# Re-timing one batch's normalisations, q projection and rotation inside a hand-ordered attention kernel

## The chip, the cores and the metric

The kernel runs on one core of one Trainium2 chip. Its engines are TensorE (PE in the profile, with its weight loads as PEld), VectorE (DVE), ScalarE (ACT), GpSimd (POOL) and SyncE (SP), which here only issues transfers. The metric is the device time of one execution in microseconds; a lower time is better.

## The reference

One pre-norm transformer layer without learned norm weights, on x of shape (8, 512, 128), all float32:

```python
x = x + attention(layernorm(x))      # 16 heads of 8 columns, rotary q and k, causal softmax
x = x + experts(layernorm(x))        # 8 experts, tokens chosen by top-k of Sinkhorn-normalised gates

q, k, v = split(xn @ W_attn)
q = q * cos + rotate_half(q) * sin   # the same for k
att = softmax(where(causal, q @ k.T / sqrt(8), -inf))
y = (att @ v) @ W_proj
```

## The kernel before

There are eight batches of 512 tokens, each kept as four tiles of 128 tokens. Attention goes through the batches in turn, and each batch through four **slots** of four heads; slot (b, s) below is slot s of batch b. In a slot, every engine goes through the same list, each taking the entries that are its own:

```python
STEP = [("w", 8), ("n", 0), ("n", 1), ("v", 0), ("u", 0), ("w", 9), ("x", 0), ("u", 1), ("u", 2),
        ("v", 3), ("u", 3), ("mx", 0), ("v", 1), ("v", 2), ("u", 4), ("c", 0), ("x", 1), ("u", 5),
        ("c", 1), ("u", 6), ("c", 2), ("x", 2), ("u", 7), ("c", 3), ("c", 4), ("c", 5), ("x", 3),
        ("ot", 0), ("c", 6), ("u", 8), ("c", 7), ("u", 9), ("x", 4)]
```

- `u0` to `u9`: score rows of the **next** slot (PE, L470); DVE takes the row maxima (L937).
- `n0`, `n1`: DVE turns the sixteen maxima of this slot into minus the maximum as a high and a low bf16 part, in NMX (L948, L951). Each is a tiny instruction.
- `mx`: PE transposes NMX (L516), ACT copies it into the rows of q (L695, "the take of mx"). No chunk of the slot can start before.
- `c0` to `c7`, and `w8`, `w9` at the start of the following slot: PE makes a chunk of transposed scores (L483), ACT takes the exponential (L735), and POOL zeroes what causality forbids (L860, `causal`). c0 and c2 have no `causal` of their own, and the others give eight of them a slot, counted z0 (c1), z1 (c3), z2 to z5 (c4 to c7), z6 (w8), z7 (w9). Chunk c6 waits for the exponential of c3, c7 for that of c4, w8 for that of c5.
- `v0`, `v3`, `v1`, `v2`: PE multiplies the previous slot's exponentials with the values (L495). v0 waits for z1, v3 and v1 for z5, v2 for z7.
- `ot` in slots 0 and 2: PE transposes the result (L503), DVE divides by the sums (L958, L963).
- `x0` to `x4`: places for other work, filled by the table EXTRAS.

The other work of a batch: `xnT` (PE transposes the normalised tiles XN, ACT copies them to XNT), `q`, `k`, `v` (projections, L527 and L535), `yT`, `proj`, `xn2T`, `logits`. After `q` or `k`, DVE makes the **turn** (L929 multiplies with cosines, L930 shuffles into TS), POOL multiplies TS with sines (L840, the **product**) and adds TC (L844, the **sum**), and the result RES is cut into three bf16 parts: ACT rounds (L729, `cut`), POOL subtracts (L848, `subtract`), and so on. SP stores the parts to DRAM (L362) and loads them back as rows of q and k (L369) for the next batch's scores. All of this goes through a single PSUM bank MB (`xnT`, `q`, `k`, `v`, `mx`, `ot`, `yT`, `proj`, `xn2T`, `logits`), which the users take strictly in the order of the list: each waits until its predecessor has been copied out.

The tables give places as (slot, kind, index), and the last number of an entry says for which batch the work is, counted from the running one. For batch 0, entries ending in 2 are kept and the others are replaced by tables FIRST_.... `normalize_x` (POOL, L832) makes tiles of XN with one instruction each, `normalize_x2` (ACT, L713) tiles of the second norm, XN2, also one instruction each, and `rstd` (POOL, L816 to L823) the scale factors that the latter needs.

Of the kernel before, what the change touches and what calls it, by code (L numbers as in the profile page):

```python
# [52 lines left out]


EXTRAS = {(0, 1): ("k", 1), (1, 1): ("yT", -1), (1, 2): ("proj", -1), (1, 3): ("v", 1),
          (2, 4): ("xnT", 2), (3, 0): ("q", 2), (3, 1): ("xn2T", -1), (3, 2): ("logits", -1)}
TURN = [i ^ 16 for i in range(32)]
ROTATE = {(3, "u", 2): (0, 2), (0, "c", 4): (1, 1)}
CUT = {(3, "c", 1): (0, 0, 2), (0, "x", 0): (0, 1, 1), (0, "c", 1): (0, 2, 1),
       (1, "x", 0): (1, 0, 1), (1, "v", 1): (1, 1, 1), (1, "c", 1): (1, 2, 1)}  # L60
SUBTRACT = {(3, "c", 5): (0, 0, 2), (0, "u", 2): (0, 1, 1), (1, "u", 2): (1, 0, 1), (1, "u", 3): (1, 1, 1)}
NORMALIZE = {(2, "u", 1): (0, 3, 2), (2, "c", 4): (3, 4, 2)}
PART_ORDER = [(0, 0), (0, 1), (0, 2), (1, 0), (1, 1), (1, 2)]

# [97 lines left out]
def build(nc, x_in, w_qkv, w_swap, w_proj, gate_w, experts, rope, tri, ident, small, out):  # L162
    ctx = ExitStack()
    with ctx:
# [643 lines left out]
        def _(pool):  # L808
# [25 lines left out]
                if hi == TB:  # L834
                    last.then_inc(xn_ready, 1)

            def rotate(w, b):
                pool.wait_ge(misc_free, BANK_TURN["qk"[w], b] + 1)
                pool.nop(nofuse=True)
                pool.tensor_tensor(TS[w][:, :], TS[w][:, :], ROPE[:, 2 * w + 1, :], ALU.mult)  # L840
                pool.drain()
                if not (isinstance(b, int) and b == 0):
                    pool.wait_ge(part[w], 3 * b)
                pool.tensor_tensor(RES[w][:, :], TC[w][:, :], TS[w][:, :], ALU.add).then_inc(resid[w], 1)  # L844
# [51 lines left out]
            for j, (b, t) in enumerate(order):  # L896
                x = X[:, TB * b + t, :]
# [408 lines left out]
```

## Time and profile before

| what | value |
|---|---|
| median of 3 runs | 486.92 us (485.73 to 487.55) |
| profiled execution, its time | 488.2 us |
| profiled execution, its span from first to last instruction | 486.5 us |
| time outside the span | 1.7 us |
| slots (3,0), (3,1), (3,2), (3,3), from n0 to n0 | 10.39, 10.77, 9.21, 11.58 us |
| slot (6,2), which has no xnT and no normalisation of x | 9.21 us |

The four slots of a batch repeat almost to the hundredth from batch 1 to batch 5, so times are given on the clock of batch 3 (175.04 to 216.99 us of the span) unless another is named. A row of the timeline has the start, the duration, the engine, the line, the operation with its tiles and shapes, and in brackets the idle time of the engine before it and what ended it.

### The profile page before, as it was taken

The numbers are of one execution on the slowest core, as the hardware profiler recorded it, in microseconds if no ns is written. First come the engines' busy times: TensorE is split into PE (matmuls) and PEld (weight loads), VectorE is DVE, ScalarE is ACT, GpSimd is POOL, SyncE is SP. The second block draws the span as 40 slices with busy tenths as digits, with TensorE's granted clock in tenths as the row PEclk, the third lists the DMA queues.
The fourth block names the chain that finished last, engine by engine and source line by source line (L and its number), as shares of the span: only waits on it lengthen the run. The fifth ranks groups of instructions, "written<-read, shape, count | busy, mean of one in ns | idle before, by whom it ended". The sixth has DMA issues, their size and how long they took to land.

```text
span 486.5 us, 9335 instructions
## 1 busy us (share of the span) xinstructions
PE 409.0 (84%) x2799; PEld 203.8 (42%) x2799; DVE 403.2 (83%) x1630; ACT 306.1 (63%) x599; POOL 245.1 (50%) x425
## 2 busy tenths in 40 slices
PE   5458887988989899898989989899999878999563
PEld 4233343444435445444544544455444433434121
DVE  6978766888798888888888888898897776996997
ACT  1002584878678787867878786788778331533871
POOL 3142773667565747766665676554344200000895
PEclk9955988999999999999999999999999977999998
DMA  8670044126117022511702341170001010100122
GB/s 256 214 183 1 34 132 96 56 77 130 55 46 165 21 84 90 112 54 67 163 6 84 104 94 59 62 164 23 2 0 64 4 44 0 44 23 22 44 65 86
DMA packets 28435, 36.85 MB, mean 76 GB/s; under 512 B 2145, under 2 KB 24225, under 8 KB 26913
## 3 DMA queue, kind: packets, MB, share of 16 engines
q1 hardware_dynamic: 27312, 34.68, 25.6%
q10 hardware_dynamic: 1072, 1.57, 1.1%
q8 instruction: 22, 0.36, 0.3%
q14 instruction: 29, 0.23, 0.2%
HBM read 19.41 MB, written 16.78 MB: 74 GB/s over the span
## 4 chain that ended last, share of the span: by engine, by line
PE 53%; DVE 15%; ACT 9%; POOL 8%; issue 7%; POOLq 3%; DMA 3%; SPq 1%; DVEq 0%; ACTq 0%
PE PVB L495 12%; PE ROWB L470 10%; PE CHB L483 8%; ACT YS L735 7%; PE MB L535 5%; POOL YS L860 4%; PE ROWB L627 3%; PE CHB L627 3%; PE MB L527 3%; POOL XN L832 3%; PE MB L503 3%; DVE YS L1227 2%; DVE CHB L1227 2%; DVE X L1233 2%; PE ROWB L680 2%
## 5 line engine op out<-in xcount | busy, mean ns | idle before, releaser
L937 DVE CUSTOM_DVE_ANT_0 JUNK<-ROWB,TRI 128x384 bf16<-128x384 f32 (+3 forms) x512 | 220.5, 484 | 41.7 <-PE ROWB L470 40.0
L735 ACT ACTIVATE YS<-CHB 128x512 f32<-128x512 f32 x320 | 172.9, 612 | 36.9 <-PE CHB L483 36.2
L860 POOL TENSOR_SCALAR_AFFINE_SELECT YS<-YS 128x256 f32<-128x256 f32 x256 | 102.1, 408 | 117.9 <-ACT YS L735 111.7
L470 PE MATMUL ROWB<-YS 96*128 96x384 bf16 (+3 forms) x512 | 122.3, 312 | 8.2 <-DVE MX L937 2.9
L483 PE MATMUL CHB<-YS 104*128 104x384 bf16 (+3 forms) x512 | 116.3, 303 | 14.7 <-ACT YS L735 13.7
L495 PE MATMUL PVB<-YS,VP 128*32 128x512 f32 (+3 forms) x1024 | 94.1, 442 | 6.8 <-POOL YS L860 6.4
L470 PEld LDWEIGHTS ROWB<-YS 96*128 96x128 bf16 x512 | 43.1, 100 | 83.7 <-DVE MX L937 47.9
L695 ACT ACTIVATE YS<-MB 8x1024 bf16<-8x1024 bf16 x32 | 32.5, 1016 | 63.0 <-PE MB L516 63.0
L483 PEld LDWEIGHTS CHB<-YS 104*128 104x128 bf16 x512 | 44.2, 98 | 46.5 <-ACT YS L735 26.3
L495 PEld LDWEIGHTS PVB<-YS,VP 128*32 128x32 f32 x1024 | 34.3, 109 | 34.5 <-POOL YS L860 22.2
L899 POOL TENSOR_TENSOR SUM<-YS 128x512 f32<-128x512 f32 x10 | 13.0, 1301 | 61.6 <-ACT YS L803 61.6
L937 DVE DVE_READ_ACCUMULATOR2_ANT MX<- 128x1 f32 x512 | 41.9, 82 | 0.0
L627 PE MATMUL CHB<-WEXP,XS 128*128 128x512 f32 x64 | 34.9, 654 | 7.8 <-DVE X L1233 7.8
L848 POOL TENSOR_TENSOR RES<-RES,PARTS 128x512 f32<-128x512 f32 x28 | 32.4, 1162 | 8.1 <-ACT PARTS L729 7.8
L627 PE MATMUL ROWB<-WEXP,XS 128*128 128x512 f32 x56 | 29.3, 639 | 3.5 <-DVE X L1233 3.5
L803 ACT ACTIVATE YS<-YS,W 128x128 f32<-128x128 f32 x80 | 24.1, 388 | 5.8 <-POOL SUM L899 4.1
L729 ACT ACTIVATE PARTS<-RES 128x512 bf16<-128x512 f32 x42 | 26.5, 631 | 0.7 <-POOL RES L848 0.5
L783 ACT ACTIVATE YS<-CHB 128x1024 f32<-128x1024 f32 x10 | 10.2, 1023 | 21.6 <-PE CHB L627 21.6
L840 POOL TENSOR_TENSOR TS<-TS,ROPE 128x512 f32<-128x512 f32 x14 | 17.9, 1279 | 8.6 <-DVE TS L930 8.6
L832 POOL TENSOR_SCALAR XN<-X,MV,RSTD 128x128 f32<-128x128 f32 x28 | 22.1, 795 | 0.2 <-issue 0.2
L783 ACT ACTIVATE YS<-ROWB 128x1024 f32<-128x1024 f32 x10 | 10.2, 1023 | 18.1 <-PE ROWB L627 18.1
L627 PEld LDWEIGHTS CHB<-WEXP,XS 128*128 128x128 f32 x64 | 11.6, 203 | 21.4 <-issue 21.3
(134 smaller groups left out, 514.2 us busy)
## 6 DMA issues: line engine op xcount, KB each, us to landing
YS<-parts_scratch SPq DMA_DIRECT2D x28, 384.0 KB, 7.0
parts_scratch<-PARTS SPq DMA_DIRECT2D x15, 384.0 KB, 2.4
parts_scratch<-PARTS SPq DMA_DIRECT2D x15, 256.0 KB, 2.1
X<-in_x SPq DMA_DIRECT2D x8, 256.0 KB, 5.0
xn_scratch<-XN2S SPq DMA_DIRECT2D x8, 256.0 KB, 2.0
XS<-xn_scratch SPq DMA_DIRECT2D x8, 256.0 KB, 2.7
out<-X SPq DMA_DIRECT2D x8, 256.0 KB, 2.3
parts_scratch<-PARTS SPq DMA_DIRECT2D x15, 128.0 KB, 1.7
```

What stands on the lines that cost most here:

```text
L470: last = pe.matmul(ROWP[BANK[u]][:, col:col + keys], QP[par][0:ROWS_K, pair, P * qb:keys], KZ[par][i % 2][0:ROWS_K, pair, 0:keys], start=T ...
L483: last = pe.matmul(CH[BANK[c]][:, col:col + n], KZ[par][i % 2][0:ALL_K, pair, P * kb:P * kb + P], QP[par][0:ALL_K, pair, P * kb:T], start= ...
L495: last = pe.matmul(PVB[32 * i:32 * i + 32, P * kb:T], VP[par][:, v:v + 32], PT[s % 2][:, c, col:col + T - P * kb], start=(kb == 0 and s % ...
L535: last = pe.matmul(MB[:, n * t:n * t + n], src[:, P * t:P * t + P], weight, start=True, stop=True)
L627: last = pe.matmul(buffer(n, half), XS[b % 2][:, P * t:P * t + P], WEXP[:, 4 * half:4 * half + 4, :].rearrange("p e o -> p (e o)"), start= ...
L695: act.activation(dst, src, ACT.Copy).then_inc(misc_free, 1)
L729: act.activation(PARTS[w][:, i, :], RES[w][:, :], ACT.Copy).then_inc(part[w], 1)
L735: act.activation(PT[s % 2][:, c, :], CH[BANK[c]], ACT.Exp).then_inc(exp_done, 1)
L832: last = pool.tensor_scalar(XN[:, t, :], X[:, n, :], MV[:, n, 0:1], RSTD[:, n:n + 1], ALU.subtract, ALU.mult)
L848: pool.tensor_tensor(RES[w][:, :], RES[w][:, :], PARTS[w][:, i, :], ALU.subtract).then_inc(resid[w], 1)
L860: pool.affine_select(out=v, in_=v, pattern=[[0, 2], [1, P]], compare_op=ALU.is_ge, fill=0.0, base=0, channel_multiplier=-1).then_inc(causa ...
L937: last = dve.tensor_tensor_reduce(out=JUNK[BANK[u]][:, col:col + n], in0=ROWP[BANK[u]][:, col:col + n], in1=TRI[:, T - n:T], scale=1.0, sc ...
```

## The change

Six parts, all of them places in the tables or the order of one engine's steps:

1. `xnT` of batch b+2 goes from the end of slot 2 (x4) to x1 of slot 2; `q` of b+2 from x0 of slot 3 to x2 of slot 2.
2. `normalize_x` for b+2, four tiles on POOL: from slot 2 (three after u1, one after c4) to two after z5 of slot 0 and two after z5 of slot 1.
3. `rotate` is split in `sine_product` and `rotate`. For q of b+2: product after c5 and sum after c7 of slot 2 (both were after u2 of slot 3). For k of b+1: product after c2 and sum after c4 of slot 0 (both were after c4). In batch 0 both stay where they were.
4. The first cut of q goes from c1 of slot 3 to v1 of slot 3, just behind the take of mx on ACT; the second from x0 of the next slot 0 to c4 of slot 3.
5. The first subtraction of q goes from c5 to c1 of slot 3, the second from u2 of the next slot 0 to c5 of slot 3.
6. `normalize_x2`: its four ACT instructions go from slot 2 (two after c1, two after c6) to just behind w9 of slot 3, ahead of the take of mx.

```diff
-          (2, 4): ("xnT", 2), (3, 0): ("q", 2), (3, 1): ("xn2T", -1), (3, 2): ("logits", -1)}
+          (2, 1): ("xnT", 2), (2, 2): ("q", 2), (3, 1): ("xn2T", -1), (3, 2): ("logits", -1)}
 TURN = [i ^ 16 for i in range(32)]
-ROTATE = {(3, "u", 2): (0, 2), (0, "c", 4): (1, 1)}
-CUT = {(3, "c", 1): (0, 0, 2), (0, "x", 0): (0, 1, 1), (0, "c", 1): (0, 2, 1),
+PRODUCT = {(2, "c", 5): (0, 2), (0, "c", 2): (1, 1)}
+ROTATE = {(2, "c", 7): (0, 2), (0, "c", 4): (1, 1)}
+CUT = {(3, "v", 1): (0, 0, 2), (3, "c", 4): (0, 1, 2), (0, "c", 1): (0, 2, 1),
        (1, "x", 0): (1, 0, 1), (1, "v", 1): (1, 1, 1), (1, "c", 1): (1, 2, 1)}
-SUBTRACT = {(3, "c", 5): (0, 0, 2), (0, "u", 2): (0, 1, 1), (1, "u", 2): (1, 0, 1), (1, "u", 3): (1, 1, 1)}
-NORMALIZE = {(2, "u", 1): (0, 3, 2), (2, "c", 4): (3, 4, 2)}
+SUBTRACT = {(3, "c", 1): (0, 0, 2), (3, "c", 5): (0, 1, 2), (1, "u", 2): (1, 0, 1), (1, "u", 3): (1, 1, 1)}
+NORMALIZE = {(0, "c", 7): (0, 2, 2), (1, "c", 7): (2, 4, 2)}
...
+FIRST_PRODUCT = {(0, "c", 4): (0, 1), (0, "x", 4): (1, 1)}
 FIRST_ROTATE = {(0, "c", 4): (0, 1), (0, "x", 4): (1, 1)}
...
-NORMALIZE2 = {(2, "c", 1): (0, 2), (2, "c", 6): (2, 4)}
+NORMALIZE2 = {(3, "w", 9): (0, 4)}
...
-            def rotate(w, b):
+            def sine_product(w, b):
                 pool.wait_ge(misc_free, BANK_TURN["qk"[w], b] + 1)
                 pool.nop(nofuse=True)
                 pool.tensor_tensor(TS[w][:, :], TS[w][:, :], ROPE[:, 2 * w + 1, :], ALU.mult)
+
+            def rotate(w, b):
                 pool.drain()
                 if not (isinstance(b, int) and b == 0):
                     pool.wait_ge(part[w], 3 * b)
...
+                        if (s, kind, i) in PRODUCT_OF[bt.b]:
+                            sine_product(*PRODUCT_OF[bt.b][s, kind, i])
                         if (s, kind, i) in ROTATE_OF[bt.b]:
                             rotate(*ROTATE_OF[bt.b][s, kind, i])
```

On POOL an entry's own `causal` comes first, then product, sum, subtraction and normalisation of the same place.

## Rows read from the trace of the kernel before

**Rows 1.** Busy time by slot: (3,2) and (3,3).
```profile
core 0: us, PE busy (x) PEld busy (x) DVE busy (x) ACT busy (x) POOL busy (x), PEclk, DMA share, GB/s
196.20:205.41 9.21, 7.72 (x73) 4.28 (x74) 8.03 (x37) 7.93 (x17) 7.79 (x16) 1.00 0.48 108
205.41:216.99 11.58, 10.94 (x91) 5.29 (x90) 8.98 (x38) 8.04 (x15) 6.21 (x10) 1.00 0.16 58
```

**Rows 2.** Timeline of PE, slots (3,2) and (3,3).
```profile
198.01 1.24 PE L495 MATMUL PVB<-YS,VP 128*32 128x384 f32 x13
...
199.41 0.38 PE L483 MATMUL CHB<-YS 104*128 104x512 bf16 x1
...
202.44 0.61 PE L503 MATMUL MB<-IDF,OT 128*128 128x128 f32 x4
...
204.59 0.63 PE L503 MATMUL MB<-IDF,XN 128*128 128x128 f32 x4 [0.66 <-POOL XN L832]
205.06 0.39 PE L483 MATMUL CHB<-YS 104*128 104x256 bf16 x2
...
206.60 0.38 PE L483 MATMUL CHB<-YS 104*128 104x256 bf16 x2
206.82 1.02 PE L527 MATMUL MB<-XNT,WQKV 128*128 128x512 f32 x2
...
209.34 0.22 PE L516 MATMUL MB<-IDB,NMX 128*8 128x128 bf16 x1 [0.39 <-DVE TS L930]
...
211.18 0.60 PE L503 MATMUL MB<-IDF,XN 128*128 128x128 f32 x4
```

**Rows 3.** Timeline of ACT, slots (3,2) and (3,3).
```profile
200.80 0.87 ACT L713 ACTIVATE XN<-X,SHIFT,RSTD 128x128 f32<-128x128 f32 x2
201.57 2.54 ACT L735 ACTIVATE YS<-CHB 128x512 f32<-128x512 f32 x5
...
207.02 0.60 ACT L735 ACTIVATE YS<-CHB 128x512 f32<-128x512 f32 x1 [0.67 <-PE CHB L483]
209.76 1.02 ACT L695 ACTIVATE YS<-MB 8x1024 bf16<-8x1024 bf16 x1 [2.15 <-PE MB L516]
211.38 0.60 ACT L735 ACTIVATE YS<-CHB 128x512 f32<-128x512 f32 x1 [0.60 <-PE CHB L483]
211.88 0.60 ACT L695 ACTIVATE XN2S<-MB 128x512 f32<-128x512 f32 x1
```

**Rows 4.** Timeline of DVE: n1 of slot (0,1), then slots (3,2), (3,3).
```profile
55.55 1.20 DVE L951 SCALAR_TENSOR_TENSOR NMX<-MX,NMX 128x16 bf16<-128x16 f32 x1
...
196.51 0.18 DVE L951 SCALAR_TENSOR_TENSOR NMX<-MX,NMX 128x16 bf16<-128x16 f32 x1
...
203.09 0.36 DVE L958 RECIPROCAL RSUM<-MB 128x32 f32<-128x32 f32 x1 [0.52 <-PE MB L503]
...
207.95 0.69 DVE L929 TENSOR_TENSOR TC<-MB,ROPE 128x512 f32<-128x512 f32 x1 [0.34 <-PE MB L527]
```

**Rows 5.** POOL: slot (0,1), end of (3,0), a norm's group, PE's wait.
```profile
55.44 1.27 POOL L840 TENSOR_TENSOR TS<-TS,ROPE 128x512 f32<-128x512 f32 x1
...
185.89 1.84 POOL L860 TENSOR_SCALAR_AFFINE_SELECT YS<-YS 128x256 f32<-128x256 f32 x5
...
L832 POOL TENSOR_SCALAR XN<-X,MV,RSTD x28: 789/792/812, 36.6 to 287.8; 128x128 f32<-128x128 f32 x28
...
187.07 0.43 PE L495 MATMUL PVB<-YS,VP 128*32 128x128 f32 x8 [1.01 <-POOL YS L860]
```

**Rows 6.** Start-up: timeline of PE in slots (0,3) and (1,0).
```profile
80.13 0.43 PE L470 MATMUL ROWB<-YS 96*128 96x512 bf16 x1 [2.26 <-issue]
...
85.88 0.38 PE L483 MATMUL CHB<-YS 104*128 104x512 bf16 x1
...
91.22 0.39 PE L470 MATMUL ROWB<-YS 96*128 96x512 bf16 x1
...
94.59 0.38 PE L483 MATMUL CHB<-YS 104*128 104x512 bf16 x1
```

More of the change, by code:

```diff
@@ L85 @@
 EXTRAS_OF = planned(EXTRAS, FIRST_EXTRAS)
+PRODUCT_OF = planned(PRODUCT, FIRST_PRODUCT)
 ROTATE_OF = planned(ROTATE, FIRST_ROTATE)
```

## The prediction

> **What bounds the kernel now.** I read the busy times of the page first: PE 84% and DVE 83% of the span, ACT 63%, POOL 50%. Neither of the first two is a plain bound, so the place of the idle time counts. The second view is busy time by slot. Slot (3,3) lasts 11.58 us for 8.98 us of DVE, 2.60 us idle, while slot (3,2) lasts 9.21 us for 8.03 [rows 1]. The third is the timeline of each engine across those two slots, which says what slot 3 waits for. There are two things. The transposes `xnT` at the end of slot 2 stand on PE until POOL has made the fourth tile (0.66 us) and push w8, v0 and u0 back, so that DVE has nothing between n1 and its first row maximum. Then `q` takes 1.02 us of PE, the turn takes DVE, and `mx` waits for the turn because it shares MB: it starts at 209.34, 1.39 us after L929 began [rows 2, 4]. ACT sits idle 2.15 us before it can take mx, and c0's exponential comes at 211.38, 5.97 us after n0 at 205.41 [rows 1, 3]. From there ACT sets the slot's end: w8 waits for the exponential of c5, and v0 and the next u0 stand behind w8.
>
> **The turn in slot 2 (parts 1 and 3).** I follow the new chain from c0 on PE to the n0 of slot 3, with delays taken from the rows. xnT starts 0.22 us after c0. ACT's take comes 0.70 us later (211.18 to 211.88) and lasts 0.60; q starts 0.05 after it. L929 starts 1.13 us after q (206.82 to 207.95). `ot` must now wait for the turn as mx did, 1.39 us. DVE's reciprocal follows ot by 0.65 us (202.44 to 203.09), and n0 follows the reciprocal by 2.32 us (203.09 to 205.41). The sum is 0.22 + 0.70 + 0.65 + 1.13 + 1.39 + 0.65 + 2.32 = 7.06 us, where before it is 6.00 us (199.41 to 205.41) [rows 1 to 4]. Slot 2 gets **1.06 us** longer.
>
> **POOL's norms ahead of slot 2 (part 2).** Each slot now has 2 x 0.79 = 1.58 us of `normalize_x` right behind z5, in front of z6 and z7 [rows 5]. This costs in two ways. First, z7 is later and v2 waits for it: z5 had ended just before n1's 196.51, and 1.58 us of norms and z6 and z7 (0.36 + 0.41) bring z7's end to about 198.8, while v2 is the last eight of the thirteen matmuls from 198.01 to 199.25 and began near 198.5 [rows 2, 4, 5]. That is 0.3 us. Second, n1. Its duration is 0.18 us alone, but in slot (0,1) it started at 55.55 inside a POOL product of 55.44 to 56.71 and lasted to 56.75 [rows 4, 5]. I take it that a POOL instruction in flight holds n0 and n1 until it ends. In slot (3,2) n1 began at 196.51, just behind z5; now a norm will be in flight until 197.21, so n1 ends near 197.23 instead of 196.69, u0 is 0.48 us late, and u3, mx, v1, v2 and c0 with it. The two costs overlap, so I take **0.47 us**; the bounds are 0.3 (only z7) and 1.3 (n0 and both norms in a row, should n0 come a little later).
>
> The Trainium skill (SBUF — State Buffer, "SBUF: two separate sides") has such a rule: the port pair that DVE and GpSimd share is an exclusive lock, held for a whole instruction, and it asks for a DVE operation with two SBUF inputs or a two-port mode and a GpSimd operation that reads SBUF. The trace agrees with it in n1's 1.20 us. By the rule the norms would block as the product did, which gives the 0.48 us; without it part 2 would cost the 0.3 us of z7 alone.
>
> **Slot 3 without q (parts 1, 4, 6).** After `ot` PE goes through c6, u8, c7, u9 to w8, an estimate of 0.44 + 4 x 0.22 = 1.32 us by the pace of w9 and q (206.60 and 206.82), and w9's exponential follows w8 by 1.96 us (205.06 to 207.02). As ot is 2.97 us ahead of n0, that exponential starts 0.31 us after n0. Behind it stand the four norms of part 6: the exponential's 0.48, then 4 x 0.385 (200.80 to 201.57 for two) = 1.54 us. So the take of mx starts 2.33 us after n0; mx itself would be ready some 0.4 us sooner, so the norms cost that much. c0's exponential follows the take by 1.62 us (209.76 to 211.38). The first cut of q falls into this gap, which had 0.60 us idle for a pitch of 0.52: no cost. c0's exponential is then 3.95 us after n0 where it was 5.97: **2.02 us** gained [rows 2, 3]. Between c0 and c5 there is one cut as before (the second, instead of the first), which leaves the gain of 2.02, less what was hidden: the take of xn2T and the logits keep their places, and PE's c1 to c3 now follow the take of xn2T as before, but cut 1 at c4 comes after PE's wait for the logits, where cut 0 at c1 was covered by it (c1 had 0.48 us of room before c2 was needed). So 0.48 us is paid that was hidden: **1.54 us** net at c5. Were the cut covered after all, it would be 2.02.
>
> POOL at the same place: z3, then one subtraction of q, then z4 and z5 for the next v3, as before; the other subtraction now lies behind z0, ahead of the wait for c3's exponential. No change. On SP nothing moves: it stores q's parts behind the save of XN2S, as before.
>
> Slots 2 and 3 together: + 1.06 + 0.47 - 1.54 = -0.01 us a batch.
>
> **Slots 0 and 1 (parts 2 and 3).** Product and sum of k stood in one row after z2, z3 to z7 followed only from 185.89 on, and v3 of slot (3,1) waited 1.01 us for z5 [rows 5]. The product at c2 lies in POOL's wait for c3's exponential, so z3 to z7 start some 1.25 us sooner (184.64) and z5 ends at 185.77. That gain is spent again: two norms hold n1 until about 186.55, where the causals held it to 186.3, and u3 must wait for u0, so mx comes 0.2 us sooner, not 1.0; z7 ends at 185.77 + 1.58 + 0.72 = 188.07 instead of 185.89 + 1.84 = 187.73; k's first subtraction follows it, and the cut behind that stands on ACT ahead of c0's exponential. Gain and loss nearly cancel there: **-0.07 us**; bounds -0.4 (norms hidden) and +0.3 (z7 and the cut both late). A batch in full is thus -0.08, and five of them (1 to 5) **-0.4 us**.
>
> **Batch 0.** In slot (0,0) two norms now stand ahead of k's rotation at x4; the chain of cuts behind it moves by about 1.0 us (1.58 less 0.5 us of room), and the loads for batch 1 too. u0 of slot (0,3), which waits for those loads after 2.26 us of idle PE, moves from 80.13 to about 81.1. The longer slot 2 is hidden in that wait. But from u0 to c0 PE took 5.75 us with q (80.13 to 85.88) and takes 3.37 us without (91.22 to 94.59) [rows 6]; there is no second norm in this batch. + 1.0 - 2.4 = **-1.4 us**; bounds -2.4 (the norms are covered) and 0 (the chain moves by all of 1.58, and PE is slow again after its wait).
>
> **Batches 6 and 7.** No xnT, q or norms of x are left. Slot (6,2) lasts 9.21 us like (3,2) (the table ahead): there the norms of ACT delay c2's exponential and so c5 and ot, and DVE stands 0.52 us before the reciprocal [rows 4]. Without them this idle time goes, and slot 3 pays 0.1 as PE is early there. -0.4 us in each batch. Batch 6 also has the earlier product without norms behind it, so half of v3's wait of 1.01 us goes (u3 then waits for u0): -0.5 us. Together **-1.3 us**.
>
> **Sum.** -0.4 - 1.4 - 1.3 = -3.1 us against the profiled execution's 488.2 us (span 486.5 plus 1.7). Taken from the median of 486.92 this is 483.8; I say **483.9 us**.
>
> **The rivals.**
>
> *The sum catches n1 in slot 3.* By the same rows, q's sum (1.27 us) after c7 is dangerous. I put z5's end at 207.02, n0 at 206.94 and the sum at 207.15. If n0 starts after z5's end, n1 finds the sum in flight and u0 moves by 1.1 us. mx comes that much later, of which ACT's norms hide 0.4 to 0.5: + 0.6 us in five batches, + 3.0, which gives **486.9 us**. The distance is 0.1 us, less than my error, but the instant behind z5, in which the queue drains, favours n1. Chance 0.2. The rule of the Trainium skill just named would make it so whenever the sum takes the pair first, and would give this time.
>
> *Start-up brings nothing*, since the delayed chain of k's cuts decides there (the bound of 0 above): **485.3 us**. For: everything in slot (0,1) hangs on that chain. Against: the 2.4 us are read from two slots that differ by q. Chance 0.1.
>
> *Slower.* n1 is caught as above and nothing hides it: ACT is behind in slot 3 anyway because the four norms, two cuts and the exponentials stand in one row, so all 1.15 us reach c5, 5 x 1.15 = 5.8 us: 483.9 + 5.8 = **489.7 us**. It decides once ACT has no idle time left ahead of the take of mx; against it stands the 2.15 us of idle time there before [rows 3]. Chance 0.13.
>
> *The change doesn't do what it says*: q's cuts earlier could bring loads forward, but k's cuts come last in SP's order and keep their places, so this is neither gain nor loss and no case of its own.
>
> *As summed*, chance 0.57, between 481.5 and 485.5: each batch may be off by 0.3 us.
>
> **How the numbers follow.** This kernel's measurement tells 0.5%, or 2.4 us, from no change, so faster means below 484.5. The summed case puts about 0.42 of its 0.57 there and the rest within. Same takes that rest, the first rival and start-up: 0.44. Slower takes its rival and a little more: 0.14. The range from 481.5 to 488.5 leaves out the slower case and a larger gain. The likeliest case's own range is 481.5 to 485.5.
>
> **What the profile would show.** Slot (3,2) near 10.7 us, slot (3,3) near 9.6 and ACT's idle time before its take of mx near zero in slot 3; n1 near 0.7 us in slots 1 and 2; n1 of slot 3 at 0.2 or, for the first rival, above 1.2; PE's wait before v3 in slot 1 gone; slot (0,3) shorter by more than 4 us, most of it moved into (0,2). The prediction is wrong if `ot` does not wait for the turn, or if n1 is not held by norms.

## The result, and the profile after

| what | before | after |
|---|---|---|
| median of 6 runs each | 486.62 us (485.73 to 487.55) | 490.06 us (488.79 to 491.28) |
| ratio to before, 95% interval | | 1.0072 (1.0051 to 1.0094) |
| profiled execution, its span | 488.2, 486.5 us | 489.57, 487.8 us |

The changed kernel is 0.7% slower, 3.44 us by the medians. Lines moved: n0 and n1 are now L955 and L958, row maxima L944, the turn's shuffle L937, chunks L486, scores L473, values L498, transposes L506 and L519, exponentials L738, the take of mx L698, cuts L732, second norm L716, `causal` L865, norms L835, product L843, sum L849, subtractions L853, loads L372.

Busy time by slot of batch 3, from n0 to n0, for the changed kernel (the columns of [rows 1]):

```profile
175.68:186.57 10.89, 10.24 (x85) 4.67 (x77) 9.92 (x41) 7.93 (x15) 6.70 (x13) 1.00 0.07 24
186.57:197.43 10.86, 10.00 (x86) 5.54 (x87) 9.21 (x43) 8.90 (x19) 7.04 (x13) 1.00 0.48 128
197.43:208.32 10.89, 10.00 (x81) 4.82 (x81) 9.43 (x40) 7.55 (x14) 7.98 (x16) 1.00 0.45 95
208.32:218.52 10.20, 8.46 (x76) 4.65 (x77) 8.58 (x36) 8.76 (x17) 5.07 (x10) 1.00 0.22 78
```

Slot (3,2) went from 9.21 to 10.89 us, slot (3,3) from 11.58 to 10.20 [rows 1], slot (3,0) from 10.39 to 10.89 and (3,1) from 10.77 to 10.86. DVE is busier in slot (3,0) than before (9.92 us for 9.42), although its list did not change there: busy time holds waiting too. The rows of DVE and POOL around n0 and n1 say what for. First DVE of the changed kernel, at n0 and n1 of slots (3,1), (3,3) and (4,0):

```profile
186.57 0.43 DVE L955 TENSOR_SCALAR NMX<-MX 128x16 bf16<-128x16 f32 x1
187.03 0.21 DVE L958 SCALAR_TENSOR_TENSOR NMX<-MX,NMX 128x16 bf16<-128x16 f32 x1
...
208.32 0.18 DVE L955 TENSOR_SCALAR NMX<-MX 128x16 bf16<-128x16 f32 x1
208.53 1.28 DVE L958 SCALAR_TENSOR_TENSOR NMX<-MX,NMX 128x16 bf16<-128x16 f32 x1
...
218.52 0.87 DVE L955 TENSOR_SCALAR NMX<-MX 128x16 bf16<-128x16 f32 x1
```

Then POOL at the same places:

```profile
185.84 1.13 POOL L865 TENSOR_SCALAR_AFFINE_SELECT YS<-YS 128x256 f32<-128x256 f32 x3
186.96 1.59 POOL L835 TENSOR_SCALAR XN<-X,MV,RSTD 128x128 f32<-128x128 f32 x2
...
189.25 1.17 POOL L853 TENSOR_TENSOR RES<-RES,PARTS 128x512 f32<-128x512 f32 x1
...
207.58 0.77 POOL L865 TENSOR_SCALAR_AFFINE_SELECT YS<-YS 128x256 f32<-128x256 f32 x2
208.51 1.26 POOL L849 TENSOR_TENSOR RES<-TC,TS 128x512 f32<-128x512 f32 x1 [0.16 <-issue]
...
218.19 1.17 POOL L853 TENSOR_TENSOR RES<-RES,PARTS 128x512 f32<-128x512 f32 x1
```

In slot 3 the sum of q starts at 208.51 and n1 at 208.53. The sum ends at 209.77, n1 at 209.81: 1.28 us for an instruction that takes 0.18. In slot 0 the second subtraction of q runs from 218.19 to 219.36 and n0 from 218.52 to 219.39. In slot 1, z5 ends at 186.97 and n0 at 187.00; but n1, started inside a norm that runs on to 187.77, ends at 187.24 after 0.21 us. So a sum, a product, a subtraction or a causal in flight holds n0 and n1 to its own end, and a norm does not hold n1: in all traces n1 inside a norm takes 0.18 to 0.21 us, in slot 1 of some batches 0.40, and ends 0.3 us or more before the norm does. No n0 started inside a norm, so nothing here shows what a norm would do to it.

PE and ACT in slots (3,2) and (3,3) of the changed kernel. PE:

```profile
200.32 0.64 PE L498 MATMUL PVB<-YS,VP 128*32 128x256 f32 x8 [0.26 <-POOL YS L865]
...
201.12 0.38 PE L486 MATMUL CHB<-YS 104*128 104x512 bf16 x1
...
205.30 0.66 PE L506 MATMUL MB<-IDF,OT 128*128 128x128 f32 x4 [0.62 <-DVE TS L937]
...
210.48 0.39 PE L473 MATMUL ROWB<-YS 96*128 96x512 bf16 x1 [1.10 <-DVE MX L944]
210.80 0.22 PE L519 MATMUL MB<-IDB,NMX 128*8 128x128 bf16 x1
```

ACT:

```profile
201.53 0.60 ACT L738 ACTIVATE YS<-CHB 128x512 f32<-128x512 f32 x1
...
209.12 1.64 ACT L716 ACTIVATE XN<-X,SHIFT,RSTD 128x128 f32<-128x128 f32 x4
211.22 1.02 ACT L698 ACTIVATE YS<-MB 8x1024 bf16<-8x1024 bf16 x1 [0.46 <-PE MB L519]
212.26 0.63 ACT L732 ACTIVATE PARTS<-RES 128x512 bf16<-128x512 f32 x1
212.92 0.60 ACT L738 ACTIVATE YS<-CHB 128x512 f32<-128x512 f32 x1
```

`ot` waits for the turn, as the prediction said. In slot 3, PE's idle 1.10 us before u3 is the held n1 passed on; mx comes 2.48 us after n0, and ACT, done with its norms, still waits 0.46 us for it.

In what follows the piece from c0's exponential in one slot to c0's exponential in the next is taken as the measure: every slot has this point once, so the pieces add up to the whole. It is read off the timeline of ACT for batch 2; "start" is where that exponential stands in slot (1,0), "five batches" from there to slot (6,0), "rest" from there to slot (7,3). The rows of the table below the first two are the experiments.

| kernel | start | 0 to 1 | 1 to 2 | 2 to 3 | 3 to 0 | five batches | rest |
|---|---|---|---|---|---|---|---|
| before | 95.01 | 10.98 | 9.96 | 11.55 | 9.44 | 210.00 | 66.30 |
| after | 94.97 | 11.07 | 10.14 | 11.39 | 9.93 | 212.95 | 65.32 |
| e1 sum later | 94.80 | 11.09 | 10.14 | 10.95 | 9.94 | 210.82 | 65.34 |
| e6 second norm back | 95.42 | 11.08 | 10.14 | 10.48 | 9.94 | 208.39 | 65.73 |
| e2 e1 and e6 | 94.98 | 11.07 | 10.14 | 10.44 | 9.93 | 208.10 | 65.76 |
| e3 norms behind z7 | 91.58 | 10.44 | 9.96 | 11.39 | 9.94 | 208.81 | 65.33 |
| e4 batch 0: norms in slot 1 | 95.49 | 11.10 | 10.13 | 11.38 | 9.93 | 212.84 | 65.33 |
| e10 batch 0: norms behind z7 | 92.88 | 11.07 | 10.14 | 11.39 | 9.94 | 212.98 | 65.32 |
| e11 second cut back | 94.16 | 11.08 | 10.13 | 11.38 | 9.33 | 209.90 | 65.32 |
| e5 e1 and e3 | 91.09 | 10.44 | 9.96 | 10.96 | 9.93 | 206.61 | 65.33 |
| e7 e5 and e6 | 93.07 | 10.43 | 9.96 | 10.44 | 9.93 | 203.98 | 65.76 |
| e8 e7 and e11 | 89.67 | 10.68 | 9.96 | 10.44 | 9.33 | 201.71 | 65.76 |
| e9 before, norms behind z7 | 93.25 | 11.47 | 9.96 | 11.05 | 9.44 | 210.07 | 66.29 |
| e12 before, product apart | 93.48 | 10.43 | 9.96 | 11.55 | 9.44 | 207.20 | 65.76 |

Two things the table does not show by itself. The five batches are alike but for one piece: in batch 3 of the changed kernel 1 to 2 takes 10.43 us and not 10.14 (10.15 for 9.96 in e3), where z5 starts 0.3 us later on POOL while the rows of PE and ACT stand where they stand in batch 2; and 3 to 0 of batch 4 takes 9.74 us and not 9.44 in the kernel before. Why is open in both; in the difference of five batches they all but cancel. And "start" is one profiled execution each, and moves from one to the next: with the norms of batch 0 ahead of z6 and z7 in both slots, as in the changed kernel, it is 94.16 to 95.42 us in five kernels, with them behind z7 of slot (0,0) 89.67 to 93.07 in five, e9 (93.25) apart, which keeps q in slot 3.

### The profile page after: what moved, and what is told of

It reads as the page before. It is cut to its first block, busy times and chain, and to the rows that moved or that the text cites. A ratio compares the mean times of both kernels' runs of the same rounds, so it can differ in the third digit from the quotient of the medians.

```text
span 487.8 us, 9335 instructions
## 1 busy us (share of the span) xinstructions
PE 410.3 (84%) x2799; PEld 200.9 (41%) x2799; DVE 410.5 (84%) x1630; ACT 307.9 (63%) x599; POOL 243.9 (50%) x425
## 4 chain that ended last, share of the span: by engine, by line
PE 52%; DVE 17%; ACT 13%; issue 6%; POOL 5%; DMA 3%; SPq 1%; DVEq 0%; POOLq 0%; ACTq 0%
PE PVB L498 12%; PE ROWB L473 11%; ACT YS L738 9%; PE CHB L486 9%; PE MB L538 5%; PE ROWB L630 3%; PE MB L506 3%; PE CHB L630 3%; PE MB L530 3%; DVE YS L1234 2%; POOL YS L865 2%; DVE JUNK L944 2%; DVE CHB L1234 2%; DVE X L1240 2%; PE ROWB L683 2%
## 5 line engine op out<-in xcount | busy, mean ns | idle before, releaser
L944 DVE CUSTOM_DVE_ANT_0 JUNK<-ROWB,TRI 128x384 bf16<-128x384 f32 (+3 forms) x512 | 221.2, 485 | 38.9 <-PE ROWB L473 36.4
L738 ACT ACTIVATE YS<-CHB 128x512 f32<-128x512 f32 x320 | 172.9, 609 | 43.6 <-PE CHB L486 43.3
L865 POOL TENSOR_SCALAR_AFFINE_SELECT YS<-YS 128x256 f32<-128x256 f32 x256 | 101.9, 410 | 131.3 <-ACT YS L738 126.2
L473 PE MATMUL ROWB<-YS 96*128 96x384 bf16 (+3 forms) x512 | 122.3, 312 | 15.1 <-DVE MX L944 10.3
L486 PE MATMUL CHB<-YS 104*128 104x384 bf16 (+3 forms) x512 | 116.4, 305 | 10.0 <-ACT YS L738 8.1
L498 PE MATMUL PVB<-YS,VP 128*32 128x512 f32 (+3 forms) x1024 | 96.4, 444 | 3.2 <-POOL YS L865 2.9
L473 PEld LDWEIGHTS ROWB<-YS 96*128 96x128 bf16 x512 | 43.8, 100 | 88.9 <-DVE MX L944 54.2
L698 ACT ACTIVATE YS<-MB 8x1024 bf16<-8x1024 bf16 x32 | 32.5, 1017 | 51.9 <-PE MB L519 51.8
L486 PEld LDWEIGHTS CHB<-YS 104*128 104x128 bf16 x512 | 44.8, 99 | 42.3 <-ACT YS L738 20.1
L498 PEld LDWEIGHTS PVB<-YS,VP 128*32 128x32 f32 x1024 | 31.0, 108 | 35.2 <-POOL YS L865 20.1
L944 DVE DVE_READ_ACCUMULATOR2_ANT MX<- 128x1 f32 x512 | 41.9, 82 | 0.0
L853 POOL TENSOR_TENSOR RES<-RES,PARTS 128x512 f32<-128x512 f32 x28 | 32.4, 1161 | 5.9 <-ACT PARTS L732 5.8
L732 ACT ACTIVATE PARTS<-RES 128x512 bf16<-128x512 f32 x42 | 26.4, 631 | 5.2 <-POOL RES L853 3.5
L835 POOL TENSOR_SCALAR XN<-X,MV,RSTD 128x128 f32<-128x128 f32 x28 | 22.2, 800 | 0.2 <-issue 0.2
L559 PE MATMUL PVB<-IDF 128*128 128x128 f32 x34 | 7.7, 422 | 15.1 <-DMA parts_scratch<-PARTS 11.2
```

The source lines that it names most:

```text
L473: last = pe.matmul(ROWP[BANK[u]][:, col:col + keys], QP[par][0:ROWS_K, pair, P * qb:keys], KZ[par][i % 2][0:ROWS_K, pair, 0:keys], start=T ...
L486: last = pe.matmul(CH[BANK[c]][:, col:col + n], KZ[par][i % 2][0:ALL_K, pair, P * kb:P * kb + P], QP[par][0:ALL_K, pair, P * kb:T], start= ...
L498: last = pe.matmul(PVB[32 * i:32 * i + 32, P * kb:T], VP[par][:, v:v + 32], PT[s % 2][:, c, col:col + T - P * kb], start=(kb == 0 and s % ...
L698: act.activation(dst, src, ACT.Copy).then_inc(misc_free, 1)
L732: act.activation(PARTS[w][:, i, :], RES[w][:, :], ACT.Copy).then_inc(part[w], 1)
L738: act.activation(PT[s % 2][:, c, :], CH[BANK[c]], ACT.Exp).then_inc(exp_done, 1)
```

## The experiments

Each is told with its median, the number of its runs, and the ratio to the kernel before on the same chip (95% interval). In the same terms the changed kernel stands at 1.0072. The edits are against the changed kernel, except for e9 and e12.

### Does the sum hold n1?

**e1_sum_later.** The sum of q goes from c7 to w9, one place further, behind n1.

```diff
-ROTATE = {(2, "c", 7): (0, 2), (0, "c", 4): (1, 1)}
+ROTATE = {(3, "w", 9): (0, 2), (0, "c", 4): (1, 1)}
```

> The changed kernel with one place moved: the sum of q's rotation (POOL, 1.27 us) stands behind z7 at the start of slot 3 (after w9) and no longer behind z5 at the end of slot 2. Theory A (the sum catches n1): n1 of slot 3 falls from 1.28 us to at most 0.3, ACT's take of mx comes about 0.55 us sooner after n0, every batch from 0 to 5 is about 0.6 us shorter, and the time falls by 3.0 to 3.6 us, to about 486.5 to 487. Theory B (the held n1 is hidden, because the four second norms stand on ACT ahead of the take anyway): n1 is short, but the time falls by less than 1 us. Theory C (the loss is in batch 0 alone): less than 1 us as well, with the batches from 1 on at 42.5 us as now.

Measured: 487.16 us (12), 1.0022 (0.9999 to 1.0045). DVE of e1 at n0 of slot (3,3):

```profile
207.30 0.42 DVE L955 TENSOR_SCALAR NMX<-MX 128x16 bf16<-128x16 f32 x1
207.75 0.18 DVE L958 SCALAR_TENSOR_TENSOR NMX<-MX,NMX 128x16 bf16<-128x16 f32 x1
```

ACT of e1 in the same place:

```profile
208.10 1.64 ACT L716 ACTIVATE XN<-X,SHIFT,RSTD 128x128 f32<-128x128 f32 x4
209.76 1.02 ACT L698 ACTIVATE YS<-MB 8x1024 bf16<-8x1024 bf16 x1
```

n1 is free and mx is 0.83 us sooner after n0 (1.65 for 2.48), but the take follows the last norm with no idle time in between, 2.46 us after n0 where it was 2.90. So the collision costs 0.44 us a batch, and ACT's norms hide the rest of the 1.1 us.

**e6_norm2_only** and **e2_sum_and_norm2.** The second norm goes back to slot 2; in e2 the sum is moved as well.

```diff
-NORMALIZE2 = {(3, "w", 9): (0, 4)}
+NORMALIZE2 = {(2, "c", 1): (0, 2), (2, "c", 6): (2, 4)}
```

> The previous kernel, and part 6 undone: the four second norms of ACT stand in slot 2 again (two after c1, two after c6). If they cost what stands ahead of the take of mx, the take comes at 0.42 us after mx in slot 3 and each of the batches 1 to 5 is 0.4 us shorter than in the previous kernel: 2 us in all, less 0.5 us each in slot 2 of batches 6 and 7, so about 1 us faster. Rival: in slot 2 they push c2 to c5 back on ACT by 0.8 us, z3, the product and z5 follow, and slot 3 loses at its front what it gains at the take: no change or up to 1 us slower.

> The changed kernel with only the second norm of ACT put back to slot 2. With the sum moved away the same edit gave 0.5 us a batch. Theory (the two costs hide one another: while n1 is held to 1.28 us, mx is ready only 2.48 us after n0, and ACT has finished the norms by then): no change in slots (1..5, 3), 11.39 from slot 2 to slot 3 stays, and batches 6 and 7 lose 0.4 us together: within 0.7 us of the changed kernel. Rival (each costs its own time wherever it stands): 0.5 us a batch, 2.5 us faster.

Measured: e2 485.23 us (12), 0.9982 (0.9964 to 1.0000), a further 0.51 us a batch; e6 486.13 us (12), 0.9989 (0.9967 to 1.0011). The expectation for e6, that either cost hides the other, did not come about: it brought 0.91 us a batch, nearly as much as e2. Here is DVE of e6 at n0 of slot (3,3):

```profile
206.94 0.30 DVE L955 TENSOR_SCALAR NMX<-MX 128x16 bf16<-128x16 f32 x1
207.27 0.18 DVE L958 SCALAR_TENSOR_TENSOR NMX<-MX,NMX 128x16 bf16<-128x16 f32 x1
```

POOL of e6:

```profile
206.80 0.41 POOL L865 TENSOR_SCALAR_AFFINE_SELECT YS<-YS 128x256 f32<-128x256 f32 x1 [0.19 <-ACT YS L738]
207.37 1.27 POOL L849 TENSOR_TENSOR RES<-TC,TS 128x512 f32<-128x512 f32 x1 [0.16 <-ACT YS L738]
```

The sum starts 0.43 us after n0 where it was 0.19, since the last causal ahead of it now waits for an exponential that stands behind two of the norms on ACT. n1 starts at 207.27 and the sum at 207.37, so n1 passes first and takes 0.18 us. n1 is passed in all five batches. So the sum catches n1 in the changed kernel only because part 6 took ACT's norms out of slot 2. The collision is a product of parts 3 and 6.

### What do the norms ahead of z6 and z7 cost?

**e3_norms_behind_z7.** All four norms go behind z7 of slot 0, in every batch.

```diff
-NORMALIZE = {(0, "c", 7): (0, 2, 2), (1, "c", 7): (2, 4, 2)}
+NORMALIZE = {(0, "w", 9): (0, 4, 2)}
```

> The changed kernel with the four normalisations of x on POOL in one group behind z7 at the start of slot 0 (after w9), where POOL is idle for some 4 us until c1, and none behind z5. If the norms ahead of z6 and z7 cost time (v2 waits for z7, and the cut of k behind it): v2 starts 0.68 us after mx in slots 1 and 2, c0's exponential comes 0.4 to 0.5 us sooner in slot 1 and 0.15 in slot 2, so 0.6 us a batch and 3 us over five; and in batch 0 the loads go out 2 us sooner, as before the change, which gives up to 2 us more: 485 to 487 in all. If POOL's norms lie beside other work (rival), the time stays within 1 us of the changed kernel.

Measured: 482.53 us (6), 0.9929 (0.9909 to 0.9950). Against the changed kernel this is 7.0 us by the ratios. Of that, 0.83 us a batch (212.95 less 208.81 in five), so that 2.8 us are left for the start; the two profiled executions show 3.4 there. Slots 0 to 1 give 0.63 and 1 to 2 give 0.18. The way in slots 0 to 1 is seen on ACT of the changed kernel in slot (3,1):

```profile
188.66 1.02 ACT L698 ACTIVATE YS<-MB 8x1024 bf16<-8x1024 bf16 x1 [0.96 <-PE MB L519]
190.45 0.63 ACT L732 ACTIVATE PARTS<-RES 128x512 bf16<-128x512 f32 x1 [0.77 <-POOL RES L853]
191.10 0.60 ACT L738 ACTIVATE YS<-CHB 128x512 f32<-128x512 f32 x1
```

and on ACT of e3:

```profile
183.77 1.02 ACT L698 ACTIVATE YS<-MB 8x1024 bf16<-8x1024 bf16 x1 [1.07 <-PE MB L519]
184.81 0.63 ACT L732 ACTIVATE PARTS<-RES 128x512 bf16<-128x512 f32 x1
```

k's subtraction at 189.25 stands behind two norms and z6, z7; the cut waits 0.77 us for it on ACT, and c0's exponential waits behind the cut. Without the norms there the cut follows the take at once.

**e12_before_product.** Against the kernel before: only k's product goes to c2, the split of part 3 for k alone.

```diff
-ROTATE = {(3, "u", 2): (0, 2), (0, "c", 4): (1, 1)}
+PRODUCT = {(3, "u", 2): (0, 2), (0, "c", 2): (1, 1)}
+ROTATE = {(3, "u", 2): (0, 2), (0, "c", 4): (1, 1)}
```

> The kernel before the change, with only k's rotation split: the product after c2 of slot 0, the sum after c4 as it was. Theory (v3 of slot 1 waited 1.0 us on PE for z5, because product and sum stood in one row ahead of z3 to z5; without norms behind z5 that gain is kept): slot 0 takes 10.44 us from exponential to exponential instead of 10.98, in batches 1 to 6, and the time falls by 3.3 us, to about 483. Rival (the wait was hidden by n1 and u0, which POOL holds longer): 1 us or less.

Measured: 482.85 us (10), 0.9926 (0.9901 to 0.9950). Slots 0 to 1 take 10.43 us for 10.98, and so it goes in six batches: 3.3 us, as expected. This part of the change is a gain by itself; in the changed kernel the norms spend it.

**e9_before_with_norms.** Against the kernel before: only the four norms of x move behind z7 of slot 0.

```diff
-NORMALIZE = {(2, "u", 1): (0, 3, 2), (2, "c", 4): (3, 4, 2)}
+NORMALIZE = {(0, "w", 9): (0, 4, 2)}
```

> The kernel before the change with one entry altered: the four normalisations of x stand behind z7 of slot 0; xnT, q, cuts and second norm as before the change. Theory (PE's wait of 0.66 us for the fourth tile at the end of slot 2 is real and ends last): xnT no longer waits, u0 of slot 3 comes 0.8 us sooner, a batch takes 41.1 to 41.2 us, five batches give 3.5 to 4 us: about 482.5. If so, the normalisations alone are worth more than the whole change lost. Rival: q's turn, standing at x0, still sets mx, and only 0.3 us a batch come through: 485.

Measured: 486.16 us (12), 0.9993 (0.9979 to 1.0007). The gain from slot 2 to 3 is there (11.05 for 11.55), and slots 0 to 1 take it all back (11.47 for 10.98). POOL of e9, end of slot (3,0):

```profile
183.38 1.26 POOL L844 TENSOR_TENSOR RES<-TC,TS 128x512 f32<-128x512 f32 x1
184.60 1.83 POOL L860 TENSOR_SCALAR_AFFINE_SELECT YS<-YS 128x256 f32<-128x256 f32 x5
```

and DVE of e9:

```profile
183.74 0.94 DVE L948 TENSOR_SCALAR NMX<-MX 128x16 bf16<-128x16 f32 x1
```

The sum ends at 184.64, n0 at 184.68. The sum of k caught n0 of slot (3,1) in the kernel before as well, but later in its flight, so that n0 took 0.54 us (at 185.43). With the norms and the subtraction ahead of z0 the sum starts later against n0, which now takes 0.94. Without product and sum in one row (e3) the same norms cost nothing.

### Where did the start go?

**e4_start_only** and **e10_start_behind_z7.** Only batch 0 has its four norms elsewhere: behind z5 of slot (0,1) in e4, behind z7 of slot (0,0) in e10.

```diff
-NORMALIZE_OF = planned(NORMALIZE, {})
+NORMALIZE_OF = [{(1, "c", 7): (0, 4, 2)}] + planned(NORMALIZE, {})[1:]   # e4
+NORMALIZE_OF = [{(0, "w", 9): (0, 4, 2)}] + planned(NORMALIZE, {})[1:]   # e10
```

> The changed kernel, with batch 0 alone altered: its four normalisations of x stand behind z5 of slot (0,1), none behind z5 of slot (0,0). If the start-up chain decides (two norms ahead of k's rotation and of z6, z7, so that v2, c0, the cuts and the loads of batch 1 are late), the last load is issued at about 72.4 us as before the change instead of 74.4, slot (1,0) begins 1.0 to 2.0 us sooner, and the time falls by as much. If only n1 held in slot (0,3) counts there, slot (1,0) begins at the same time as in the changed kernel, within 0.3 us.

> The changed kernel, batch 0 alone altered: its four normalisations of x stand behind z7's place at the start of slot (0,0) (after w9), where POOL has nothing to do. Batches 1 to 5 as in the changed kernel. Theory (the start-up's share of the loss is the two pairs of norms ahead of z6 and z7, the first in (0,0), the second in (0,1)): slot (1,0) begins 3.4 us sooner, as it did when the norms of all batches were moved, and the time falls by 3.4 us to about 486.5. Rival (the loads' landing sets slot (0,3), and it varies from run to run by as much): less than 1 us in the median.

Measured: e4 488.91 us (8), 1.0050 (1.0032 to 1.0068), which is not told from the changed kernel's 1.0072 (1.0051 to 1.0094); e10 487.03 us (12), 1.0016 (0.9992 to 1.0040), which is. PE of the changed kernel in slot (0,1) shows what they are about:

```profile
60.36 1.08 PE L498 MATMUL PVB<-YS,VP 128*32 128x256 f32 x8 [2.68 <-POOL YS L865]
61.37 0.61 PE L473 MATMUL ROWB<-YS 96*128 96x384 bf16 x2
```

and POOL of the changed kernel:

```profile
55.37 1.57 POOL L835 TENSOR_SCALAR XN<-X,MV,RSTD 128x128 f32<-128x128 f32 x2
56.91 1.27 POOL L843 TENSOR_TENSOR TS<-TS,ROPE 128x512 f32<-128x512 f32 x1
58.32 1.26 POOL L849 TENSOR_TENSOR RES<-TC,TS 128x512 f32<-128x512 f32 x1
59.53 0.77 POOL L865 TENSOR_SCALAR_AFFINE_SELECT YS<-YS 128x256 f32<-128x256 f32 x2
```

v2 waits 2.68 us for z7, which stands behind two norms, product and sum. Busy time of the changed kernel in the stretch behind it:

```profile
60.00:65.00 5.00, 4.64 (x21) 1.97 (x22) 2.65 (x13) 2.55 (x6) 2.98 (x4) 0.50 0.22 79
65.00:70.00 5.00, 4.92 (x26) 3.31 (x28) 1.57 (x11) 3.95 (x11) 3.35 (x5) 0.58 0.30 105
```

The granted clock is 0.50 there, PE's lower level (1.2 GHz), and 0.58, the lower level for most of the stretch, and two chunk or score matmuls take 0.61 to 0.63 us for 0.38. What the clock costs can be read from e1, which has the same batch 0 but for q's sum: it waited 2.93 us at this place and was granted 0.69 and 0.97. From the start of v2 to the loads for batch 1 it took 10.66 us (61.44 to 72.10), where the changed kernel took 12.08 (60.36 to 72.44). So 1.4 us are the clock's; e2, e6 and e11, which were granted 0.50 and then 0.51 to 0.60, took 12.1 too. In e10 the norms have left that row. Busy time of e10:

```profile
60.00:65.00 5.00, 3.29 (x27) 2.32 (x26) 2.54 (x17) 4.52 (x13) 4.62 (x7) 1.00 0.52 184
65.00:70.00 5.00, 5.00 (x50) 1.97 (x49) 4.30 (x19) 4.52 (x9) 2.42 (x7) 1.00 0.29 79
```

The clock stays at 1.00 in these stretches and batch 1 begins 2.1 us sooner (92.88 for 94.97); by the ratios e10 is 2.7 us better, where 3.4 was expected. Part of what the norms gave went again in slot (0,3): the clock is 0.74 between 80 and 85 us in e10, and from u0 to c0 it took 4.79 us, for 3.26 in e3, e5 and e8, where it was 1.00. e4 failed as a remedy (batch 1 begins at 95.49, not sooner): the four norms ahead of z6 and z7 in slot (0,1) hold v2 of slot (0,2) in turn. PE of e4:

```profile
72.27 0.64 PE L498 MATMUL PVB<-YS,VP 128*32 128x256 f32 x8 [2.13 <-POOL YS L865]
```

### What does the earlier second cut cost?

**e11_cut_only.** The second cut of q and the second subtraction go back to where they were before.

```diff
-CUT = {(3, "v", 1): (0, 0, 2), (3, "c", 4): (0, 1, 2), (0, "c", 1): (0, 2, 1),
+CUT = {(3, "v", 1): (0, 0, 2), (0, "x", 0): (0, 1, 1), (0, "c", 1): (0, 2, 1),
...
-SUBTRACT = {(3, "c", 1): (0, 0, 2), (3, "c", 5): (0, 1, 2), ...
+SUBTRACT = {(3, "c", 1): (0, 0, 2), (0, "u", 2): (0, 1, 1), ...
```

> The changed kernel with only q's second cut and subtraction put back to x0 and u2 of the next slot 0. Theory (ACT's row from c0 to c5 sets the end of slot 3): 9.93 us from exponential to exponential in slot 3 falls to 9.3 to 9.45, slot 0 pays up to 0.25, net 0.25 to 0.5 us in each of five batches: 1.3 to 2.5 us faster than the changed kernel. Rival (in the changed kernel n1 and POOL set slot 0's front, so a sooner c5 is lost in front of n0, which a POOL instruction holds): within 0.5 us.

Measured: 485.65 us (12), 0.9976 (0.9956 to 0.9997). Slots 3 to 0 take 9.33 us for 9.93, and nothing is paid in slot 0. DVE of e11 at n0 of slot (4,0):

```profile
216.44 0.21 DVE L955 TENSOR_SCALAR NMX<-MX 128x16 bf16<-128x16 f32 x1
```

The gain is not where the cut was. From c0's exponential of slot (3,3) to n0 of slot (4,0) it takes 5.60 us in the changed kernel (212.92 to 218.52) and 5.61 before (211.38 to 216.99) [rows 1, 3], and 5.59 in e11, which has no cut between the two (210.85 to 216.44): the cut at c4 is hidden. What is gone in e11 is the 0.66 us by which the subtraction held n0. The two were moved together, so how much a subtraction without the delay of the cut would hold was not tried.

### Together

**e5_sum_and_norms** (e1 and e3), **e7_sum_norms_norm2** (with e6's edit), **e8_and_cut** (with e11's edit as well).

> The changed kernel with both moves at once: q's sum behind z7 of slot 3, the four normalisations of x behind z7 of slot 0. Theory (the two costs are separate and add): by the slots already measured a batch takes 10.44 + 9.96 + 10.95 + 9.93 = 41.3 us from c0's exponential to c0's exponential, against 41.9 before the change and 42.5 with it; the time is about 480.5. Rival (with the norms out of the way z5 comes earlier or later and the sum or another POOL instruction catches n1 in a new place): 41.7 us a batch and 482 to 483, as with the norms moved alone.

> The previous kernel with the second norm of ACT back in slot 2. Theory: the 0.5 us that it gave in front of the take of mx comes on top: 40.8 us a batch, about 478.5. Rival: with everything else gone from slot 2's front, ACT is the next bound there and the two pairs of norms between the exponentials delay c5 and z3 to z5: less than 1 us gained.

> The previous kernel, and q's second cut and subtraction back at x0 and u2 of the next slot 0. Slot 3 measured 9.93 us from exponential to exponential in every variant with the cut at c4, and 9.44 before the change. Theory (the cut at c4 costs its full 0.48 us because w8 waits for c5's exponential and z5 for z3): slot 3 falls to 9.45 and the time by 2.4 us, 0.5 in each of five batches. Rival: at x0 of slot 0 the cut and at u2 the subtraction (1.17 us on POOL behind z7 and next to the four norms) delay z0 or the take of mx there, and slot 0 gives the gain back: within 0.5 us.

Measured: e5 481.04 us (6), 0.9891 (0.9869 to 0.9914); e7 479.50 us (6), 0.9844 (0.9819 to 0.9869); e8 475.82 us (6), 0.9777 (0.9753 to 0.9801). e8 beats the kernel before by 2.2% (2.0 to 2.5) and the changed one by 2.9%. Busy time by slot of e8, batch 3:

```profile
166.48:176.98 10.50, 9.30 (x80) 4.70 (x77) 9.30 (x40) 8.05 (x15) 9.31 (x14) 1.00 0.11 37
176.98:187.22 10.24, 9.90 (x89) 5.92 (x87) 9.34 (x43) 8.90 (x19) 5.81 (x13) 1.00 0.51 137
187.22:197.83 10.61, 9.99 (x82) 5.16 (x81) 9.66 (x41) 8.78 (x18) 6.27 (x15) 1.00 0.45 96
197.83:207.08 9.25, 8.85 (x80) 4.65 (x77) 7.63 (x35) 7.45 (x14) 5.80 (x11) 1.00 0.20 71
```

The batch takes 40.60 us where before took 41.95. The pieces are those of the single edits in slots 1 to 3 (9.96, 10.44, 9.33). Slots 0 to 1 take 10.68 for 10.43, so 0.25 us of the gain is given back, in the way that the rival named. In slot (3,0) of e8 the second subtraction (171.41 to 172.57) stands behind z7 and four norms, and ACT's third cut waits for it ahead of the exponentials of c2 to c5:

```profile
172.61 0.63 ACT L732 ACTIVATE PARTS<-RES 128x512 bf16<-128x512 f32 x1 [0.49 <-POOL RES L853]
```

In e7 the third cut follows the exponential of c1 without a wait, and n0 of slot 1 comes 6.56 us after c0's exponential, where it comes 6.76 after it in e8.

## Why the prediction was wrong

The forecast was 483.9 us, 3.1 less than before, and the time rose by 3.44 to 490.06. By the pieces from c0's exponential to c0's exponential, each term of the prediction can be set beside what it measured.

| term | forecast | measured | from |
|---|---|---|---|
| norms in front of slot 2 (1 to 2) | +0.47 | +0.18 | 9.96, 10.14 in batch 2; given back whole in e3 |
| turn chain in slot 2 | +1.06 | +1.20 | c0 on PE to n0: 6.00 before, 201.12 to 208.32 after |
| slot 3 without q, nothing caught | -2.02 | -1.81 | c0's exponential 5.97 us after n0, 4.16 in e1 |
| sum catches n1 | 0 (rival: 0.6) | +0.44 | 4.60 after, 4.16 in e1 |
| cut and subtraction (3 to 0) | +0.48 | +0.49 | 9.44, 9.93 |
| slots 0 and 1 (0 to 1) | -0.07 | +0.09 | 10.98, 11.07 |
| a batch | -0.08 | +0.60 | five: 210.00, 212.95 |
| batches 6 and 7 | -1.3 | -1.0 | 66.30, 65.32 |
| batch 0 | -1.4 | +1.5 | see below |

Five batches are +2.95 us, the rest -0.98. The start of the two profiled executions is equal (95.01 and 94.97), but the execution of before was 1.6 us above its median and that of after 0.5 below, and e12, which has the same batch 0 as before, reaches the same point at 93.48 in an execution that is at its median. (Behind slot (7,3)'s c0 exponential, before's execution takes 115.2 us to the end of the span, and those of after and e12 114.6 and 114.7, which is the other part of its 1.6 us.) So I put the start at +1.5, an estimate from single executions; 2.95 - 0.98 + 1.5 = 3.5, where the medians say 3.44.

**The step that failed first is batch 0**, "+ 1.0 - 2.4 = -1.4", off by 2.9 us. The +1.0 did not hold. Against e12, whose batch 0 is that of the kernel before, u0 of slot (0,3) moved from 78.70 to 82.00, so the term measured +3.3. I let the two norms delay only k's cuts. They also stand ahead of z7, which v2 of slot (0,1) waits for, for 2.68 us, and behind that wait PE was granted its lower clock. The loads for batch 1 went out at 72.44 us, where it was 69.08 in e12 (70.45 in the execution of before); 1.4 of these 3.4 us are the clock's, by the comparison with e1, and I put the rest down to the wait with what hangs on it, which was not measured apart. The -2.4 came about in number: from u0 to c0 of slot (0,3) the changed kernel takes 3.41 us (82.00 to 85.41) for 5.75 [rows 6]. But it was in good part luck. I read it from two slots that differ by q, and they differ by the granted clock as well (0.66 between 80 and 85 us, 1.00 between 90 and 95). Without q but at 0.74 and 0.67, in e10 and e7, the same stretch takes 4.79 and 4.85 us, and 3.26 in seven others at 1.00. So q is worth about 0.9 us there and the clock about 1.5. My sum took the higher clock for granted and had the other only in the bound of 0; that the changed kernel got it there is luck. The same delay that I priced in slot 2 as "0.3 us of z7" was nine times as large where product and sum stood in the same row, and I did not work it out there. e10 shows what the norms of batch 0 alone cost: 2.1 us of the start by the trace, 2.7 by the ratio. I also took both of [rows 6] from an execution whose start was late, as e12 shows.

**The second is the sum's place.** The rival "the sum catches n1 in slot 3" happened, in every one of the five batches, at a chance of 0.2 (0.33 with the slower rival, which has it too). Its rule was right, its size nearly so (0.44 for 0.6), the distance was judged wrongly. I had n0 0.08 us ahead of z5's end and the sum behind both, with 0.1 us in favour of n1; it came to 0.02 us against it. Such a distance is nothing that a sum of ten durations can tell, and 0.2 was too little for what is nearly an even chance. e6 adds that I never asked what moves the sum: for batches 1 to 5 I costed the norms of part 6 in slot 3 alone, and in slot 2 they would have delayed the sum past n1.

**The third is "I take it that a POOL instruction in flight holds n0 and n1 until it ends"** for norms. It holds for product, sum, subtraction and causal, and not for n1 inside a norm: n1 of 187.03 lasted 0.21 us inside one. That was one of the two signs that I had named for the prediction being wrong. So slot 2's front costs only what z7 costs, +0.18 us (in batch 4 the thirteen matmuls that end with v2 take 1.42 us, for 1.24 in [rows 2]), below the 0.3 of the lower bound. In batch 3, whose row of PE shows 0.26 us of waiting before v2, the whole difference is 0.47 us, the number forecast, but by a late z5 and z7 and not by a norm that holds n1: luck. The rule of the Trainium skill that I set beside it (SBUF — State Buffer, "SBUF: two separate sides") counts every GpSimd operation that reads SBUF; the rows agree for tensor_tensor and the causals and disagree for the norm, a tensor_scalar that reads SBUF, and the measurement decides.

**Right in size by luck, wrong in cause:** "0.48 us is paid that was hidden" for the cut at c4. The cut stayed hidden; the second subtraction, of which I wrote "no change", holds n0 of the next slot 0 for 0.66 us more than it needs (0.36 us in all in the kernel before, 0.87 now). By my own rule for n1 I should have looked at what POOL has in flight at each n0, not at slot 3's alone.

**Right for nearly the right reason:** `ot` behind the turn (1.20 for 1.06), slot 3 without q (1.81 for 2.02, and with ACT's norms binding it, as e1 shows), and slots 0 and 1, where the product's gain of 0.55 (e12) and the norms' loss of 0.63 (e3) cancel as forecast. Of the two ways that I had named for that loss, n1 held by the norms was not there, and k's cut on ACT, which waits behind the norms, was the one. In batches 6 and 7 the earlier product brought 0.54 us (e12; forecast 0.5), and the norms of ACT gone from slot 2 brought 0.42 in both together (65.34 in e1, 65.76 in e2; forecast 0.8).

The slower rival asked that all 1.15 us reach c5; 0.44 did. The kernel is slower all the same, by the first rival and the start together, a case that I had not made.

## What to carry to other kernels

Before placing a long instruction on an engine that can hold another's, write down for each short instruction of that other engine what would be in flight at its start; where the distance is below a few tenths of a us, count it as even chances, and move the long one past it (here one place, 0.44 us a batch). Put movable work behind the last instruction that somebody waits for, not ahead of it, and price it again in every slot whose row is fuller than the one looked at: here two norms cost 0.18 us in slot 2, two cost 0.63 by way of slot 1, and the four of batch 0 cost 2.7 at the start. And try the parts of a bundled change one by one, also on the kernel before: the product alone brought 0.7%, while the bundle lost that much.

## What was not expected of the hardware

- n0 and n1, on 16 elements a partition, end 0.03 to 0.04 us after the POOL instruction in flight when that is a tensor_tensor or an affine_select; started inside a tensor_scalar with scalars for each partition, n1 takes 0.18 to 0.21 us, at times 0.40, with 0.71 to 0.78 us of that instruction still to run.
- Which of the two starts first decides, at 0.02 us: n1 at 208.53 against the sum at 208.51 cost 1.1 us; in e6 n1 at 207.27 and the sum at 207.37 cost nothing.
- After a wait of 2.68 us PE's granted clock was 0.50 and 0.58 in the next two stretches of 5 us; in e1, after 2.93 us at the same place, 0.69 and 0.97; in e10, with a longest wait of 1.72 us in the slot, 1.00. So the length of the wait alone does not tell it.
- The two ends of the program are not steady, where the pieces in between repeat within 0.1 us from one execution to the next. From c0's exponential of slot (7,3) to the end of the span it took 113.9 to 116.4 us in the fourteen profiled executions, although no edit touches that stretch. And the same batch 0 reached c0's exponential of slot (1,0) at 95.01 us in the profiled execution of before and at 93.48 in that of e12. The granted clock differs too. Busy time of before in that stretch:

```profile
60.00:65.00 5.00, 3.27 (x20) 2.15 (x19) 2.84 (x16) 4.20 (x8) 4.62 (x5) 0.82 0.52 184
```

and of e12:

```profile
60.00:65.00 5.00, 3.28 (x27) 2.20 (x25) 2.57 (x16) 4.52 (x12) 4.62 (x6) 1.00 0.52 184
```
